# Adding the output bias before instead of after the values of the later token tiles, in the first slot of a cross-attention block

## What is computed

```python
q  = layer_norm(query, ln1_g, ln1_b) @ wq + bq        # 16 heads of 32
k  = context @ wk + bk
v  = context @ wv + bv
p  = softmax(where(allowed, q k^T / sqrt(32), -inf))  # 64 keys per sequence
x1 = query + (p v) @ wo + bo
h  = layer_norm(x1, ln2_g, ln2_b)
out = x1 + gelu(h @ w1 + b1) @ w2 + b2
```

## Time and profile before

| what | before |
|---|---|
| median of 3 runs | 1868.11 us |
| lowest and highest of them | 1867.82 and 1868.26 us |
| span of the profiled execution, first to last instruction | 1864.5 us |
| TensorE's matmuls, busy | 1799.3 us (97%) |
| VectorE, busy | 1247.9 us (67%) |
| ScalarE, busy | 640.5 us (34%) |
| GpSimd, busy | 443.8 us (24%) |
| mean granted TensorE clock | 0.982 |

### The profile page before, as it was taken

The page is one execution under the profiler, slowest core; times in us unless marked ns, Lnnn a source line. Parts: engine busy times, 40 slices in busy tenths (PEclk is TensorE's granted clock), DMA queues, the critical chain, the costliest instruction groups (busy, mean ns, idle before and its releaser), DMA issues.

```text
span 1864.5 us, 26584 instructions
## 1 busy us (share of the span) xinstructions
PE 1799.3 (97%) x10213; PEld 819.6 (44%) x10213; DVE 1247.9 (67%) x1930; ACT 640.5 (34%) x799; POOL 443.8 (24%) x376
## 2 busy tenths in 40 slices
PE   6678899999999999999999999999999999999999
PEld 3233344444444444444444444444444444444444
DVE  6767757667675767757676676757677576866622
ACT  5654424242232424223242422324242232424211
POOL 2523114131320314122141313203141221413200
PEclk8878999999999999999999999999999999999999
DMA  8230232314123241412323131332413133231200
GB/s 288 54 105 12 46 91 46 91 23 79 35 60 77 46 91 23 78 36 57 80 46 91 19 81 38 57 80 46 91 21 77 40 57 79 46 91 19 50 23 23
DMA packets 287738, 116.27 MB, mean 62 GB/s; under 512 B 262616, under 2 KB 264192, under 8 KB 287616
## 3 DMA queue, kind: packets, MB, share of 16 engines
q1 hardware_dynamic: 287616, 114.61, 27.4%
HBM read 31.22 MB, written 16.78 MB: 26 GB/s over the span
## 4 chain that ended last, share of the span: by engine, by line
PE 90%; DVE 5%; POOL 1%; ACT 1%; DMA 1%; issue 1%; SPq 0%; DVEq 0%; ACTq 0%
PE ff_ps L1141 34%; PE ff_ps L1384 34%; PE at_ps L1141 18%; PE at_ps L1298 2%; PE at_ps L1318 1%; DVE w_all L829 1%; POOL arena L560 1%; DVE arena L829 0%; DVE xhat L818 0%; DMA arena<-in_L_xattn_wk 0%; PE ff_ps L1213 0%; DVE arena L1114 0%; DVE arena L1061 0%; PE at_ps L1213 0%; DVE smax L1059 0%
## 5 line engine op out<-in xcount | busy, mean ns | idle before, releaser
L1141 PE MATMUL ff_ps<-arena,w_all 128*128 128x512 f16 x3072 | 701.8, 381 | 2.3 <-DVE arena L829 2.3
L1384 PE MATMUL ff_ps<-w_all,arena 128*128 128x512 f16 x3072 | 698.0, 379 | 0.9 <-DVE arena L829 0.9
L1141 PEld LDWEIGHTS ff_ps<-arena,w_all 128*128 128x128 f16 x3072 | 300.4, 98 | 371.7 <-issue 15.6
L1384 PEld LDWEIGHTS ff_ps<-w_all,arena 128*128 128x128 f16 x3072 | 294.4, 98 | 358.6 <-issue 6.4
L753 ACT ACTIVATE arena<-ff_ps,b1p,scales 128x512 f32<-128x512 f32 x256 | 198.5, 775 | 634.6 <-PE ff_ps L1141 634.3
L1114 DVE TENSOR_SCALAR arena<-arena,scales 128x512 f16<-128x512 f32 x256 | 150.1, 586 | 215.6 <-ACT arena L753 215.5
L829 DVE SCALAR_TENSOR_TENSOR arena<-arena,scales 128x512 f16<-128x512 f32 x256 | 239.2, 934 | 9.1
L511 POOL TENSOR_TENSOR rstd<-ve,minus_half 128x1 f32<-128x1 f32 x128 | 85.6, 669 | 561.1 <-DVE ve L801 561.1
L555 POOL TENSOR_TENSOR x_sb<-x_sb,bo_row 128x512 f32<-128x512 f32 x64 | 92.6, 1477 | 359.8 <-PE at_ps L1298 350.5
L687 ACT ACTIVATE norm_hl<-xhat 128x512 f16<-128x512 f32 x120 | 73.9, 628 | 287.6 <-DVE xhat L818 287.6
L560 POOL TENSOR_TENSOR arena<-arena,rsum 128x1024 f32<-128x1024 f32 x64 | 124.8, 1971 | 176.1 <-DVE rsum L1087 176.1
(11 more groups left out here) (154 smaller groups left out, 1377.3 us busy)
## 6 DMA issues: line engine op xcount, KB each, us to landing
x_sb<-in_x SPq DMA_DIRECT2D x64, 256.0 KB, 2.8
out_x<-arena SPq DMA_DIRECT2D x64, 256.0 KB, 2.1
w_all<-in_L_xattn_w SPq DMA_DIRECT2D x6, 1024.0 KB, 11.6
arena<-in_L_xattn_w SPq DMA_DIRECT2D x2, 1024.0 KB, 15.8
v_sb<-v_sb SPq DMA_DIRECT2D x6, 192.0 KB, 3.0
arena<-in_ctx SPq DMA_DIRECT2D x1, 1024.0 KB, 5.2
arena<-in_L_xattn_wk SPq DMA_DIRECT2D x1, 1024.0 KB, 7.4
arena<-in_L_xattn_wq SPq DMA_DIRECT2D x1, 1024.0 KB, 7.4
```

The source lines that it names most:

```text
L1141: last = nc.tensor.matmul(out_ap, s, m, start=(i == 0), stop=(i == n - 1))
L1384: last = nc.tensor.matmul(ff2_ps[:, t, :], pair[:, s, rows], m[:, j], start=(j == 0 and i == 0), stop=(j == NJ - 1 and i == 2))
```

## The change

In slot 0, GpSimd waits for the bias rows and adds bo to the four residual tiles right after it has copied this chunk's values, ahead of the value bias and low half of token tiles 1 to 3. The wait for all moves of values stays behind these; after it come the reciprocal roots. Nothing else is changed.

```diff
@@ -583,12 +583,12 @@
                         normalise(t)
                     pool.wait_ge(v_moved, 6 * 16)
                     batch_values()
+                    pool.wait_ge(rows_loaded, 2 * 16)
+                    add_bo()
                     for n in range(1, KT):
                         values_bias(n)
                         values_low(n)
                     pool.wait_ge(v_moved, 12 * 16)
-                    pool.wait_ge(rows_loaded, 2 * 16)
-                    add_bo()
                 else:
```

## The result

The changed kernel took 1871.19 us (median of 12 runs, 1869.83 to 1873.21) against 1867.64 us for the kernel before in the same measurement (12 runs, 1866.03 to 1869.01). The ratio is 1.0020, with a 95% interval of 1.0012 to 1.0028: slower by some 3.5 us (2.2 to 5.2), where 5.6 was forecast. The forecast time of 1873.7 is 2.5 above the measured one; half a microsecond of that is the kernel before, whose median fell from 1868.11 to 1867.64 with more runs. The lower end of the range, 1871.3, was missed by 0.1. The measured 3.5 also lies just under the 3.74 us that the prediction took for the least a measurement can tell from none, a region to which it gave a chance of 0.17; by the interval found here the change is real all the same.

The account below looks back on a forecast made before the run. TensorE, busy 97% of the span, was taken as the bound, with late values gating it in the first slot. Removed wait 0 + later values 5.60 + clock 0 = 5.60 us, giving 1873.7 us; range 1871.3 to 1875.4.

Parts of the forecast that it names:

- The lower end of the range: Whole kernel: 1871.3 us, from the values' lower delay of 3.76 us less half a microsecond of clock.
- the least a measurement can tell from none: Whole kernel: a change of 0.2%, 3.74 us; chance 0.17 that the time stays the same by this bound.
- Where the delay enters: Slot 0, GpSimd: four adds ahead of the values cost 6.80 us, 1.20 comes back, third Y step 5.60 later.
- The upper bracket: Slot 0: each add stands still for one whole VectorE instruction, 1.96 us each, values 6.64 us later.
- the full-lock rival: Slot 0: each GpSimd add waits out a whole 0.70 us VectorE instruction; +6.64 us, 1874.7 us; chance 0.13.
- an instruction already running is rarely met at its start: Slot 0, GpSimd beside VectorE: argument against adds each losing a whole 0.70 us VectorE instruction.
- The wait that is removed: Slot 0, VectorE's first residual add: its 5.16 us wait, some 1.2 from the bias, is worth 0; TensorE covers it.
- The side chain over the w2 loads: Slot 0: last w2 loads, ScalarE's weight sums and their transpose go 5.6 us later; next bound if the projection came sooner.
- If each is drawn from the same four rows the sum does not change on average, so I take 0: TensorE's four stretches at 1.2 GHz: clock effect taken as 0, with -2.85 to +1.02 us kept for the range.
- if the four slow stretches of TensorE differ in sum by over 2 us: Changed profile, TensorE's four stretches at the lower clock: a sum differing by over 2 us would show the prediction wrong.
- The rival that has the clock give back part: TensorE's slow stretches: three rise sooner, 2.0 to 2.85 us return, leaving 2.75 to 3.6; 1870.9 to 1871.7 us; chance 0.14.
- stands 3.6 above that span: Whole kernel before: median of runs 1868.11 us against the profiled span of 1864.5; added to 1870.1 to give 1873.7.

Follow-up runs that it names:

- e1: Against the kernel before: the four bo adds stay behind the values but go ahead of the wait for all moves of values; ratio 1.0001 (0.9992 to 1.0009).
- e2: Against the kernel before: the bo adds and their wait moved to the front of slot 0, right behind key_blocks(), where GpSimd idles; ratio 0.9997 (0.9989 to 1.0006).
- e3: Against the kernel before: four adds nobody reads put at the place of the change, the real adds left behind the values; ratio 1.0023 (1.0013 to 1.0032).
- e4: Against the kernel after: ScalarE evicts the first V pair ahead of the second and third Y steps; ratio to the kernel before 1.0022 (1.0014 to 1.0031).

## Why the prediction was right and where it was not

*Where the delay enters: right.* The adds took 6.66 us for a forecast 6.80, and the values behind them ran at the undisturbed 1.26 and 1.15; the third Y came 5.45 us later for a forecast 5.60. The upper bracket, 6.64, was not reached: 1.67 for an add lies between the undisturbed 1.24 and the 1.96 of a full stand-still. So the price of the full-lock rival falls, but not its mechanism. The reason given against it, that "an instruction already running is rarely met at its start", is not what the rows show: the two engines take turns, one instruction of each, and a turn of VectorE's costs an add 0.43 us and not 0.70.

*The wait that is removed is worth 0: right*, shown by e1 and e2. The reason given, that TensorE covers it, depends on TensorE's slow start; e3 shows the bias holding the residual adds once that start is shorter.

*The side chain over the w2 loads shifts with the rest and is the next bound: right*, shown by TensorE's waits for the weight sums, 0.97 us in the kernel after and 2.12 in e4.

*"If each is drawn from the same four rows the sum does not change on average, so I take 0": this step failed.* The four durations are not drawn anew. In all 14 profiles the granted clock falls 0.03 to 0.66 us after the copies end, so that every execution comes to the change at nearly the same place against the clock's falls and rises, and a given delay meets the same rise each time, or one of two neighbours. For four adds all four slow stretches were shorter, and 1.3 to 1.7 us came back. The prediction had named this as a sign of being wrong, "if the four slow stretches of TensorE differ in sum by over 2 us"; they differ by 3.36. The rival that has the clock give back part (2.75 to 3.6 us left) had the chance of 0.14; the measured 3.5 lies in it, and the 4.1 of the two profiles between it and the forecast, since less came back than the 2.0 to 2.85 us that it had priced. That the time lies so near the lower end of the range is partly luck: that end, 1871.3, was worked out for undisturbed adds with half a microsecond of clock, while the adds cost nearly what was forecast and the clock gave the rest.

*"stands 3.6 above that span": the difference is right, its reading ahead of the prediction (that the runs also hold what lies around the first and the last instruction) only half so.* The profiled execution after took 1872.47 us with a span of 1870.7, so some 1.8 lies around a span. The profiled execution of before was one of the shorter ones: the other half of the 3.6 is the difference between executions that shows in when the copies end. The forecast change of 5.60 us does not hang on it.

What stays open: why the setup ahead of the copies varies by 2.5 us between executions was not tried; whether five adds have exactly two ends rests on two profiles; and since most kernels have a single profile, how often an execution of one falls to a neighbouring group is not known.

## What to carry to other kernels

A wait in the list of waits is worth what the waiting engine's successors would gain, not its length; ask of the engine that runs on without a gap. Work moved ahead of a chain delays the chain by its time in full wherever that engine is the late one (5.45 us here), and where a chain leaves by two ways (here to V and to the weight loads) look at both, since relieving one may only lengthen the wait for the other. Where short busy stretches of TensorE start at the lower clock, a small delay may cost nothing or a whole group, so try a few sizes of it before judging an order by one.

## What was not expected

A delay was passed on in groups: 2.56 us cost nothing in the end of the span, 4.22 to 5.45 cost the same 3.6 to 4.3, and 6.66 cost either that or 3 us more, in the same kernel. GpSimd's adds and VectorE's low halves of wo took turns, one instruction of each: an add took 1.67 us for 1.24, and one of VectorE's, once the adds had begun, 1.75 for 0.70.
